# Outputs in two places beside the ring, stored four images at a time, in a group-norm and masked batch-norm kernel on one core

## The chip, the cores and the metric

The kernel runs on one core of a Trainium2 chip. A core has TensorE (PE), VectorE (DVE), ScalarE (ACT), GpSimd (POOL) and SyncE (SP), each with an instruction queue of its own, and 16 DMA engines that all queues share. Here SyncE issues the loads and ScalarE the stores. The metric is the device time of one execution in microseconds (us); lower is better.

## What is computed

The input x is 16 images x 64 channels x 256 x 256, float32, 268 MB. The reference, cut to what matters:

```
def _gn(v, G=32, eps=1e-5):            # mean and variance over each image's group of two channels
    ...
    return ((g - m) / jnp.sqrt(s + eps)).reshape(v.shape)

def _L0_conv_ref(x):                   # masked batch norm, the mean is not subtracted
    x1 = x.sum(axis=1)                 # sum over the 64 channels
    m = x1 != 0
    mean = (sum over images and places where m) / total
    var = (sum of (x - mean)^2 where m) / total
    inv = 1.0 / jnp.sqrt(var + 1e-3)
    out = jnp.where(m[:, None, :, :], x * inv, x)
    ...

x = x + _L0_conv_ref(_gn(x))
```

So each element becomes x plus its group-normed value times a number of its channel, if the sum over all 64 normed channels at its pixel isn't zero. The kernel writes outputs as if no sum were zero, counts the zeros beside it, and has a general path behind a branch (`general`, and its parts on the other engines) for the case that there are any. With these inputs the branch isn't taken.

## The kernel before

**Units and tiles.** The work is cut into 32 units, one for each group of two channels, over all 16 images. In SBUF a unit stands as 128 partitions (2 channels x 64 pieces of the picture) x 16 images x 1024 elements. A tile is four images of a unit, 2 MB. A unit has four tiles (`UNIT_TILES`), loaded in four DMAs and stored in four. There are 128 tiles.

**The ring.** `slots` has ten places of a tile. The first eight (`RING`) hold the tiles in turn, so two units at a time; tile j is in place j % 8. An output is written over its input (`out_in_ring`), except for the first four images of the last unit, which go to place 8 (`APART_PLACE`). Place 9 holds the map of zeros of the last unit. Otherwise the two places are not used in the main path.

**The engines' work on a unit u:**
- SyncE (`load`, L249) loads tile after tile. From the ninth on it waits until the store of the tile eight before it, which stood in the same place, has landed (`stored`). At the end it stores the last unit, image by image (L265 to 267).
- VectorE takes the statistics of every block of 512 elements (`block_stats`, L511), then makes means, scales and biases (`statistics`). Between the steps of that chain it does the first six blocks of the next unit (`meanwhile`), so the chain waits also for the next unit's first tile. The chain passes through small matmuls on PE (L420, L430, L431) and two square roots on ScalarE (L388, L390), and ends with `out_scale` and `out_bias`.
- TensorE (`channel_sums`) adds up the normed channels at each pixel. For 12 of the 16 images the sum goes to one of three banks of PSUM (`flush`), for 4 it stays in PSUM over all units (`stay`).
- ScalarE (`unit` at L386) goes image by image: `take` (L373) copies a flush bank to SBUF, `put_out` (L376) makes the output of an image, and after the first image of the next tile `store` (L382) issues the DMA of the tile before. It waits for an image's sum before it makes the output in place, since TensorE reads the input.
- GpSimd makes the weights and adds up what `take` copied (L349).

All loops are written out by hand, two units a turn, and each engine's order is that of its own code; semaphores hold them together. `out_ready` counts outputs, `image_summed` counts TensorE's sums, `taken` the takes.

Of the kernel before, what the change touches and what calls it, by code (L numbers as in the profile page):

```python
# [16 lines left out]
BLK = 512  # L17
HALVES = 2
TILE_IMAGES = 4
RING = 8  # L20
PLACES = 10
# [4 lines left out]
LAP = 2  # L26


def norm_conv_kernel(nc: bass.Bass, x: bass.AP, out: bass.AP):
# [52 lines left out]
    with ctx:  # L82
# [6 lines left out]
        def sem(name):  # L89
# [46 lines left out]

        APART_PLACE, NOT_ZERO = RING, RING + 1
        not_zero = slots[:, NOT_ZERO * TILE_N:NOT_ZERO * TILE_N + B * BLK // 4].bitcast(U8).rearrange(
            "p (k n) -> p k n", k=B)
# [18 lines left out]
        stored = [sem(f"stored{i}") for i in range(RING)]  # L158
# [13 lines left out]
        out_ready = sem("out_ready")  # L172
        counted = sem("counted")
# [36 lines left out]
        def out_in_ring(u, i):  # L210
            return in_place(APART_PLACE)[:, i, :] if u == LAST and i < APART else image_in_ring(u, i)
# [7 lines left out]
        def wait_for_sum(engine, u, i, it=None):  # L219


            engine.wait_ge(image_summed, in_turn((u * B + sum_order(u).index(i) + 1) * BLOCKS, it, B * BLOCKS))

        def bank_of(u, i):
            return flush[(u * ADDS + flush_order(u).index(i)) % FLUSH_BANKS][:, :]
# [4 lines left out]
        def wait_for_bank(engine, u, i, it=None):  # L230


            if u < LAST:
                engine.wait_ge(taken, in_turn(taken_with(u, i), it, ADDS))
            else:
                engine.wait_ge(compared, flush_order(u).index(i) + 1)

        def wait_for_all_stores(engine):
            for j in range(TILES - RING, TILES - UNIT_TILES):
                engine.wait_ge(stored[j % RING], 16 * (j // RING + 1))  # L240
# [5 lines left out]
        def _(sp):  # L246

            def load(j, it=None):
                if j >= RING:  # L249
                    sp.wait_ge(stored[j % RING], 16 * (j // RING) if it is None else it * 16 + 16 * (j // RING))  # L250
# [9 lines left out]
            sp.wait_ge(stored[(TILES - 1) % RING], 16 * ((TILES - 1) // RING))  # L260
# [4 lines left out]
            for i in range(B):  # L265
                sp.wait_ge(out_ready, LAST * B + i + 1)
                sp.dma_start(out_rows[LAST, :, i, :], out_in_ring(LAST, i)).then_inc(last_stored, 16)
# [34 lines left out]
        def _(pool):  # L302
# [23 lines left out]
            def unit(u, it=None):  # L326
# [9 lines left out]
                for part in sorted(parts, key=lambda part: sum_order(u).index(part[0])):  # L336
# [410 lines left out]
```

## Time and profile before

| | before |
|---|---|
| median of 3 runs | 1353.27 us |
| lowest and highest | 1345.78 and 1357.33 us |
| the profiled execution, its time | 1357.61 us |
| its span, first to last instruction | 1355.9 us |
| busy: DVE, ACT, PE, POOL | 58%, 60%, 54%, 40% of the span |
| loads | 127 DMAs of 2048 KB, median 14.2 us from issue to landing |
| stores from ScalarE | 124 DMAs of 2048 KB, median 14.7 us |
| stores of the last unit, from SyncE | 16 DMAs of 512 KB, median 5.0 us |

The busy share of an engine is the time in which it worked on something. For the DMA engines, "9" in a slice means that they were busy for 90% of it or more; that says nothing of how fast they moved, which the row of GB/s tells. "From issue to landing" includes the time in which a DMA stands in the queue behind others.

### The profile page before, as it was taken

Reading aid. Unit: us, or ns where it says so; the run is one execution under the profiler, and the core shown is the slowest. Engines: PE = TensorE matmul, PEld = TensorE weight load, DVE = VectorE, ACT = ScalarE, POOL = GpSimd, SP = SyncE. Lnnn points to the kernel's source line nnn. Section 1 sums busy time; section 2 is a strip of 40 time slices with the busy share of each in tenths; the row PEclk is TensorE's granted clock in tenths of the full one; section 3 lists DMA queues with packets and bytes.
Section 4 is the critical chain, followed back from the end, with each engine's and each line's share of the span. In section 5 each row is a group of like instructions: output and inputs, shape, how many; then the busy total and the mean of one; then the engine's idle time right before and its main releaser. Section 6 shows DMA issues by size and latency. Waiting matters only on the chain.

```text
span 1355.9 us, 13270 instructions
## 1 busy us (share of the span) xinstructions
PE 736.0 (54%) x2882; PEld 295.1 (22%) x2882; DVE 780.4 (58%) x1892; ACT 816.5 (60%) x950; POOL 547.1 (40%) x568
## 2 busy tenths in 40 slices
PE   0666345654556545466454664446645366535566
PEld 0222111221212222122111222112222122212222
DVE  7566554655546555466654665545765357555474
ACT  0775457654577545675456764567645576546766
POOL 0053344443444434454343543435434354334441
PEclk9987678876787767887667886778767787667888
DMA  9899999999999999999999999999999999999998
GB/s 378 344 404 398 421 392 394 391 394 419 390 396 388 393 420 403 397 389 396 420 392 398 399 403 413 393 396 389 397 420 388 392 384 398 389 421 389 401 416 338
DMA packets 135418, 536.99 MB, mean 396 GB/s; under 512 B 4336, under 2 KB 4336, under 8 KB 135408
## 3 DMA queue, kind: packets, MB, share of 16 engines
q1 hardware_dynamic: 69936, 276.83, 52.8%
q10 hardware_dynamic: 65472, 260.05, 47.4%
q8 instruction: 3, 0.05, 0.0%
q14 instruction: 7, 0.06, 0.0%
HBM read 268.44 MB, written 268.44 MB: 396 GB/s over the span
## 4 chain that ended last, share of the span: by engine, by line
DMA 58%; PE 17%; issue 9%; DVE 7%; ACT 6%; SPq 1%; DVEq 0%; ACTq 0%
DMA slots<-in_x_dram 33%; DMA out_dram<-slots 25%; PE flush L456 9%; ACT slots L376 5%; PE small_ps L420 3%; ACT fresh L373 1%; PE stay L452 1%; PE small_ps L430 1%; PE stay L453 1%; PE small_ps L431 1%; DVE stats L511 1%; DVE dev L556 1%; DVE by_image L541 1%; DVE spread L530 1%; DVE dev L528 1%
## 5 line engine op out<-in xcount | busy, mean ns | idle before, releaser
L511 DVE BATCH_NORM_STATS2 stats<-slots 128x6 f32<-128x512 f32 x1024 | 630.7, 679 | 522.4 <-DMA slots<-in_x_dram 519.4
L376 ACT ACTIVATE slots<-slots,out_bias,out_scale 128x1024 f32<-128x1024 f32 x512 | 622.4, 1246 | 1.6 <-DVE out_bias L567 1.3
L349 POOL TENSOR_TENSOR sums<-fresh,sums 128x512 f32<-128x512 f32 x360 | 459.5, 1276 | 333.5 <-ACT fresh L373 333.5
L456 PE MATMUL flush<-slots,weights 128*64 128x512 f32 x1536 | 441.8, 696 | 40.2 <-ACT fresh L373 39.0
L373 ACT ACTIVATE fresh<-flush,group_bias 128x512 f32<-128x512 f32 x360 | 247.6, 688 | 52.7 <-PE flush L456 52.7
L420 PE MATMUL small_ps<-spread,group_avg 128*128 128x64 f32 x64 | 21.8, 443 | 380.4 <-DVE spread L530 380.4
L388 ACT ACTIVATE by_image<-by_image,eps 128x16 f32<-128x16 f32 x32 | 9.8, 307 | 325.3 <-DVE by_image L534 324.5
L456 PEld LDWEIGHTS flush<-slots,weights 128*64 128x64 f32 x1536 | 128.6, 156 | 296.9 <-issue 149.9
L329 POOL COPY group_mean<-mean_now 128x16 f32 (+1 forms) x32 | 7.0, 220 | 448.4 <-DVE group_bias L547 448.4
L452 PE MATMUL stay<-slots,weights 128*64 128x512 f32 x512 | 139.1, 605 | 0.0
L453 PE MATMUL stay<-minus_mean,weights 128*64 128x512 f32 x512 | 138.1, 593 | 0.0
L420 PEld LDWEIGHTS small_ps<-spread,group_avg 128*128 128x128 f32 x64 | 15.8, 307 | 385.7 <-DVE spread L530 385.7
L390 ACT ACTIVATE col<-small_ps,eps 128x1 f32<-128x1 f32 x32 | 8.4, 261 | 149.8 <-PE small_ps L431 149.8
L323 POOL TENSOR_TENSOR weights<-pair_sum,rstd_now 128x256 f32<-128x256 f32 (+1 forms) x128 | 74.4, 608 | 0.0
L453 PEld LDWEIGHTS stay<-minus_mean,weights 128*64 128x64 f32 x512 | 49.4, 137 | 61.1 <-issue 61.1
L452 PEld LDWEIGHTS stay<-slots,weights 128*64 128x64 f32 x512 | 44.5, 141 | 82.0 <-issue 82.0
L420 PE MATMUL small_ps<-col,chan_avg 128*128 128x1 f32 x64 | 18.8, 362 | 74.2 <-DVE dev L494 74.2
L420 PE MATMUL small_ps<-stats,group_avg 128*128 128x64 f32 x64 | 16.0, 338 | 72.5 <-DVEq L523 72.5
L430 PE MATMUL small_ps<-col,chan_avg 128*128 128x1 f32 x64 | 18.7, 362 | 45.0 <-DVE spread L494 45.0
L420 PEld LDWEIGHTS small_ps<-col,chan_avg 128*128 128x128 f32 x64 | 16.0, 311 | 80.2 <-DVE dev L494 80.2
L420 PEld LDWEIGHTS small_ps<-stats,group_avg 128*128 128x128 f32 x64 | 10.8, 212 | 98.7 <-DVEq L523 56.5
L430 PEld LDWEIGHTS small_ps<-col,chan_avg 128*128 128x128 f32 x64 | 16.0, 310 | 47.8 <-DVE spread L494 47.8
(54 smaller groups left out, 244.6 us busy)
## 6 DMA issues: line engine op xcount, KB each, us to landing
slots<-in_x_dram SPq DMA_DIRECT2D x127, 2048.0 KB, 14.2
out_dram<-slots ACTq DMA_DIRECT2D x124, 2048.0 KB, 14.7
out_dram<-slots SPq DMA_DIRECT2D x16, 512.0 KB, 5.0
slots<-in_x_dram SPq DMA_DIRECT2D x4, 512.0 KB, 6.9
```

What stands on the lines that cost most here:

```text
L323: return pool.tensor_tensor(weights[:, u % 2, first:first + n, :], matrix.unsqueeze(1).to_broadcast([P, n, ROWS]), rstd_now[:, u % 2, firs ...
L349: pool.tensor_tensor(into, fresh[:, k % FRESH_BUFS, :], into, ALU.add).then_inc(added, 1)
L373: nc.scalar.activation(into, bank_of(u, i), ACT.Identity, bias=group_bias[:, u % 2, i:i + 1]).then_inc(taken, 1)
L376: nc.scalar.activation(out_in_ring(u, i), image_in_ring(u, i), ACT.Identity, bias=out_bias[:, u % 2, i:i + 1], scale=out_scale[:, u % 2, i ...
L420: nc.tensor.matmul(out_, lhsT, rhs, start=True, stop=True).then_inc(small_out, 1)
L430: nc.tensor.matmul(bn_var_ps, chan_avg[:, :], var_sum, start=True, stop=False)
L431: nc.tensor.matmul(bn_var_ps, chan_avg[:, :], shifted_sum, start=False, stop=True).then_inc(small_out, 1)
L452: nc.tensor.matmul(into, weight, source, start=u == 0, stop=False)
L453: nc.tensor.matmul(into, weight, minus_mean[:, u % 2, i:i + 1].to_broadcast([P, BLK]), start=False, stop=u == LAST).then_inc(image_summed, 1)
L456: nc.tensor.matmul(into, weight, source, start=True, stop=True).then_inc(image_summed, 1)
L511: last = V.bn_stats(stats[:, u % 2, k * BLOCK_STATS:(k + 1) * BLOCK_STATS], source)
L528: link(V.tensor_tensor(dev[:, :, :], means, over_folds(mean), ALU.subtract))
```

## The change

The ring of eight places stays for inputs alone. Places 8 and 9 become two output places of four images each (`out_places`). `put_out` of units 0 to 30 writes there: images 0 to 3 and 8 to 11 of each unit to the one, 4 to 7 and 12 to 15 to the other. Before the first image of four, ScalarE waits until the store that was issued last from that place has landed (`wait_for_out_places`). `store` sends one output place to HBM, again four images, 2 MB. A new semaphore `tile_free` counts the tiles whose outputs are made and whose sums are done; ScalarE raises it in `free`, right behind the store, and the load waits for it and no longer for a store. `put_out` comes ahead of `take`, as it need not wait for the sum any more.

In the last unit, outputs of images 0 to 13 go to the ring places of the unit before, and 14 and 15 to the first output place. The map of zeros moves to ring space of the unit before, and VectorE begins to count once all outputs of the units before are made. The last unit's order of images, which was 4 to 15 and then 0 to 3, becomes 0 to 15.

The core of the diff:

```diff
+STORE_IMAGES = 4
...
-    APART = TILE_IMAGES
-
-    def sum_order(u):
-        return list(range(B)) if u < LAST else list(range(APART, B)) + list(range(APART))
-
-    def flush_order(u):
-        return [i for i in sum_order(u) if i in flushed]
+    OUT_PLACES = (PLACES - RING) * TILE_IMAGES // STORE_IMAGES
+    UNIT_STORES = B // STORE_IMAGES
+    USES = UNIT_STORES // OUT_PLACES
+    ASIDE = B - 2
...
-        def out_in_ring(u, i):
-            return in_place(APART_PLACE)[:, i, :] if u == LAST and i < APART else image_in_ring(u, i)
+        def out_places(k):
+            at = RING * TILE_N + k * STORE_IMAGES * N
+            return slots[:, at:at + STORE_IMAGES * N].rearrange("p (i n) -> p i n", i=STORE_IMAGES)
+
+        def out_place(u, i):
+            if u < LAST:
+                return out_places(i // STORE_IMAGES % OUT_PLACES)[:, i % STORE_IMAGES, :]
+            return out_places(0)[:, i - ASIDE, :] if i >= ASIDE else image_in_ring(LAST - 1, i)
...
+            def wait_for_place(j, it=None):
+                sp.wait_ge(tile_free, in_turn(j - RING + 1, it, UNIT_TILES))
+
             def load(j, it=None):
                 if j >= RING:
-                    sp.wait_ge(stored[j % RING], 16 * (j // RING) if it is None else it * 16 + 16 * (j // RING))
+                    wait_for_place(j, it)
                 sp.dma_start(in_ring(j), in_dram(x_rows, j, it)).then_inc(loaded[j % RING], 16)
...
-            def store(u, t, it):
-                j = u * UNIT_TILES + t
-                act.wait_ge(out_ready, in_turn((j + 1) * TILE_IMAGES, it, B))
-                act.dma_start(in_dram(out_rows, j, it), in_ring(j)).then_inc(stored[j % RING], 16)
+            def wait_for_out_places(u, k, it):
+                n = u * UNIT_STORES + k
+                if n >= OUT_PLACES:
+                    act.wait_ge(stored[k % OUT_PLACES], in_turn(16 * (n // OUT_PLACES), it, 16 * USES))
+
+            def store(u, k, it):
+                act.wait_ge(out_ready, in_turn(u * B + (k + 1) * STORE_IMAGES, it, B))
+                at = slice(k * STORE_IMAGES, (k + 1) * STORE_IMAGES)
+                if it is None:
+                    into = out_rows[u, :, at, :]
+                else:
+                    into = out_rows[bass.ds(it * LAP + u, 1), :, at, :].rearrange("o p i n -> (o p) i n")
+                act.dma_start(into, out_places(k % OUT_PLACES)).then_inc(stored[k % OUT_PLACES], 16)
+
+            def free(u, t, it):
+                wait_for_sum(act, u, (t + 1) * TILE_IMAGES - 1, it)
+                act.sem_inc(tile_free, 1)
...
                 act.wait_ge(scale_ready, in_turn((u + 1) * 2, it, 2))
+                if u == LAST:
+                    wait_for_sum(act, LAST - 1, B - 1)
                 for i in range(B):
-                    if u < LAST or i >= APART:
+                    if u < LAST and i % STORE_IMAGES == 0:
+                        wait_for_out_places(u, i // STORE_IMAGES, it)
+                    if u == LAST and i == ASIDE:
+                        act.wait_ge(stored[0], 16 * LAST * USES)
+                    put_out(u, i)
+                    if u < LAST and i in flushed:
                         wait_for_sum(act, u, i, it)
-                    if u < LAST and i in flushed:
                         take(u, i, it)
-                    put_out(u, i)
+                    if u < LAST and i and i % STORE_IMAGES == 0:
+                        store(u, i // STORE_IMAGES - 1, it)
                     if u < LAST and i and i % TILE_IMAGES == 0:
-                        store(u, i // TILE_IMAGES - 1, it)
+                        free(u, i // TILE_IMAGES - 1, it)
                 if u < LAST:
-                    store(u, UNIT_TILES - 1, it)
+                    store(u, UNIT_STORES - 1, it)
+                    free(u, UNIT_TILES - 1, it)
...
+            dve.wait_ge(out_ready, LAST * B)
+            for i in range(B):
                 count(i)
```

How the instructions stand on ScalarE, inside the loop over units, from the fourth image of a unit to the first image's neighbour after the store. `slots<-slots` is `put_out`, `fresh<-flush` is `take`; rows without an operation on data (ISA, REGISTER_ALU) compute or hold a wait. Before:

```order
L376 ACTIVATE slots<-slots,out_bias,out_scale 128x1024 [waits image_summed]
L222 REGISTER_ALU
L372 REGISTER_ALU [waits image_summed]
L373 ACTIVATE fresh<-flush,group_bias 128x512 [waits added]
L376 ACTIVATE slots<-slots,out_bias,out_scale 128x1024
L381 ISA
L382 ISA [waits out_ready]
L382 DMA out_dram<-slots 128x4x1024
```

And in the changed kernel, at the same place:

```order
L389 ACTIVATE slots<-slots,out_bias,out_scale 128x1024
L389 ACTIVATE slots<-slots,out_bias,out_scale 128x1024 [waits stored1]
L230 REGISTER_ALU
L385 REGISTER_ALU [waits image_summed]
L386 ACTIVATE fresh<-flush,group_bias 128x512 [waits added]
L400 ISA
L406 ISA [waits out_ready]
L406 DMA out_dram<-slots 128x4x1024
L230 REGISTER_ALU
L389 ACTIVATE slots<-slots,out_bias,out_scale 128x1024 [waits image_summed]
```

The output of the fifth image has moved ahead of its take and has a wait for `stored1` on it; the DMA of the first four images stands behind both. The same rows come again with `stored0` after the eighth image and with `stored1` after the twelfth.

On SyncE, the first two loads of a turn of the loop before:

```order
L251 ISA [waits stored0]
L251 DMA slots<-in_x_dram 128x4x1024
L251 ISA [waits stored1]
L251 DMA slots<-in_x_dram 128x4x1024
```

And in the changed kernel:

```order
L264 ISA [waits tile_free]
L264 DMA slots<-in_x_dram 128x4x1024
L259 REGISTER_ALU
L264 ISA [waits tile_free]
L264 DMA slots<-in_x_dram 128x4x1024
```

The loads stand in the same order, each behind a wait for ScalarE's `tile_free` where a wait for the store of its place was.

## Rows read from the trace of the kernel before

**Rows 1.** The page, busy time by engine and the slices of the span.

```profile
span 1355.9 us, 13270 instructions
PE 736.0 (54%) x2882; PEld 295.1 (22%) x2882; DVE 780.4 (58%) x1892; ACT 816.5 (60%) x950; POOL 547.1 (40%) x568
...
DMA  9899999999999999999999999999999999999998
...
DMA packets 135418, 536.99 MB, mean 396 GB/s; under 512 B 4336, under 2 KB 4336, under 8 KB 135408
```

**Rows 2.** Waits, who for whom: total us, times, longest; SyncE's queue last.

```profile
DVE stats L511 <- DMA slots<-in_x_dram: 519.4, 80, 14.9
...
SPq L251 <- DMA out_dram<-slots: 1199.2, 119, 26.8
```

**Rows 3.** The chain that ended last: start us, us, what; ten of its pieces.

```profile
45.61 6.64 DMA out_dram<-slots
52.44 14.85 DMA slots<-in_x_dram
...
83.53 10.28 DMA out_dram<-slots
93.99 14.94 DMA slots<-in_x_dram
...
125.13 13.72 DMA out_dram<-slots
...
506.99 9.29 DMA out_dram<-slots
516.45 13.78 DMA slots<-in_x_dram
...
546.76 13.49 DMA out_dram<-slots
560.43 14.44 DMA slots<-in_x_dram
...
591.29 9.53 DMA out_dram<-slots
```

**Rows 4.** Busy time in seven stretches; last columns: PE clock, DMA share, GB/s.

```profile
45.60:1305.70 1260.10, 690.98 (x2704) 276.08 (x2702) 717.42 (x1741) 770.72 (x901) 528.43 (x531) 0.75 1.01 398
46.50:51.90 5.40, 5.40 (x28) 2.39 (x27) 5.40 (x10) 5.40 (x7) 0.00 (x0) 1.00 0.97 388
52.80:57.30 4.50, 3.34 (x16) 0.82 (x14) 1.32 (x3) 4.50 (x6) 0.00 (x0) 1.00 1.01 338
86.00:88.40 2.40, 2.40 (x13) 0.89 (x10) 2.10 (x4) 2.40 (x4) 1.97 (x2) 1.00 1.02 331
511.00:519.00 8.00, 6.75 (x32) 2.07 (x31) 4.99 (x9) 8.00 (x9) 5.10 (x4) 1.00 1.03 419
524.00:544.00 20.00, 8.43 (x24) 3.85 (x26) 12.71 (x40) 6.22 (x10) 5.97 (x9) 0.50 1.02 417
546.90:551.00 4.10, 4.10 (x22) 1.77 (x20) 3.62 (x7) 4.10 (x6) 2.88 (x3) 1.00 0.99 281
```

**Rows 5.** Timeline, DMA issues and activations: start us, us, engine line.

```profile
51.86 0.38 ACTq L382 DMA_DIRECT2D out_dram<-slots  x1
...
58.11 0.38 ACTq L382 DMA_DIRECT2D out_dram<-slots  x1
...
83.53 0.40 ACTq L382 DMA_DIRECT2D out_dram<-slots  x1
...
84.10 0.37 SPq L251 DMA_DIRECT2D slots<-in_x_dram  x1
...
89.75 0.39 ACTq L382 DMA_DIRECT2D out_dram<-slots  x1
...
1305.66 0.38 ACTq L382 DMA_DIRECT2D out_dram<-slots  x1
...
1324.40 0.38 ACTq L382 DMA_DIRECT2D out_dram<-slots  x1
...
1330.38 4.64 ACT L376 ACTIVATE slots<-slots,out_bias,out_scale 128x1024 f32<-128x1024 f32 x4 [1.25 <-DVE out_bias L567]
```

**Rows 6.** DMA issues at 51.86, 58.11, 84.10 and 89.75: last column, us to landing.

```profile
out_dram<-slots ACTq DMA_DIRECT2D x1, 2048.0 KB, 9.1
...
out_dram<-slots ACTq DMA_DIRECT2D x1, 2048.0 KB, 15.0
...
slots<-in_x_dram SPq DMA_DIRECT2D x1, 2048.0 KB, 14.4
...
out_dram<-slots ACTq DMA_DIRECT2D x1, 2048.0 KB, 15.1
```

More of the change, by code:

```diff
@@ L157, in norm_conv_kernel @@
         loaded = [sem(f"loaded{i}") for i in range(RING)]
-        stored = [sem(f"stored{i}") for i in range(RING)]
+        stored = [sem(f"stored{i}") for i in range(OUT_PLACES)]
         summed = sem("summed")
@@ L172, in norm_conv_kernel @@
         out_ready = sem("out_ready")
+        tile_free = sem("tile_free")
         counted = sem("counted")
@@ L219, in wait_for_sum @@
         def wait_for_sum(engine, u, i, it=None):
[L222 removed]
+            engine.wait_ge(image_summed, in_turn((u * B + i + 1) * BLOCKS, it, B * BLOCKS))
         def bank_of(u, i):
[L225 removed]
+            return flush[(u * ADDS + flushed.index(i)) % FLUSH_BANKS][:, :]
         def taken_with(u, i):
@@ L235, in wait_for_bank @@
             else:
-                engine.wait_ge(compared, flush_order(u).index(i) + 1)
+                engine.wait_ge(compared, flushed.index(i) + 1)
         def wait_for_all_stores(engine):
-            for j in range(TILES - RING, TILES - UNIT_TILES):
-                engine.wait_ge(stored[j % RING], 16 * (j // RING + 1))
+            for k in range(OUT_PLACES):
+                engine.wait_ge(stored[k], 16 * LAST * USES)
             engine.wait_ge(last_stored, 16 * B)
@@ L259, in _ @@
                 load(j)
-            sp.wait_ge(stored[(TILES - 1) % RING], 16 * ((TILES - 1) // RING))
+            wait_for_place(TILES - 1)
             for i in range(TILE_IMAGES):
@@ L335, in unit @@
                 parts = [list(range(w * EVERY, (w + 1) * EVERY)) for w in range(WEIGHT_PARTS)]
-                for part in sorted(parts, key=lambda part: sum_order(u).index(part[0])):
+                for part in sorted(parts, key=lambda part: part[0]):
                     if u < LAST:
@@ L433, in channel_sums @@
             def channel_sums(u, it=None):
-                for at, i in enumerate(sum_order(u)):
+                for at, i in enumerate(range(B)):
                     if u < LAST:
@@ L446, in channel_sums @@
                             before = (m - FLUSH_BANKS) // ADDS
-                            wait_for_bank(pe, before, flush_order(before)[(m - FLUSH_BANKS) % ADDS], it)
+                            wait_for_bank(pe, before, flushed[(m - FLUSH_BANKS) % ADDS], it)
                     for k in range(BLOCKS):
@@ L605, in count @@
                                            accum_out=n_part[:, i:i + 1]).then_inc(compared, 1)
-            for i in sum_order(LAST):
+            dve.wait_ge(out_ready, LAST * B)
+            for i in range(B):
                 count(i)
```

12 lines of the change are left out of this document (6 added, 6 removed).

## The prediction

> **What bounds the kernel now.** I read the page's busy rows first [rows 1]: no compute engine is busy for more than 60% of the span, while the 16 DMA engines show 9 tenths in nearly every slice. They move 536.99 MB in 1355.9 us, 396 GB/s. The windows say what they can do [rows 4]: 417 GB/s in 524 to 544 us, with loads and stores in flight together, 419 in 511 to 519 with stores alone, but 398 over the 1260.1 us from the first store of unit 0 to the first store of unit 30. So the DMA engines are always busy and run 4 to 5% below what they reach at best. Those 1260.1 us are 30 units, **42.00 us a unit**. A unit loads 8.39 MB and stores 8.39 MB; at 417 GB/s that is 40.2 us.
>
> The waits and the chain show what paces it [rows 2, 3]. VectorE waits 519.4 us for loads. SyncE's queue waits 1199.2 us for stores: a load may only go when the store of the same place, two units older, has landed. The chain is the same ring each time: store out (9.29 us from issue to landing), load in (13.78), about 16.5 us of statistics and first outputs, the next store at 546.76. That is 39.8 us; the next turn has 13.49 and 14.44 us and takes 44.5. Their mean is the 42 us.
>
> **What the change takes away.** The store leaves this ring. A load now waits for `tile_free`, which ScalarE raises when a tile's outputs are made. The old ring would then be 14 + 16.5, some 31 us a unit, and bounds nothing. The bytes, the number of DMAs and the activations stay as they are, so below 40.2 us a unit there is nothing to win: a bound of 30 x 1.8 = 54 us.
>
> **What it adds.** Outputs go to two places, and `put_out` of a tile's first image waits until the store before last has landed. The order listing of ScalarE shows more: the row that waits for `stored1` (or `stored0`) stands ahead of the previous tile's DMA. Call a unit's stores A, B, C, D. B isn't issued until A has landed, C not until B has landed, and the next unit's A not until D has landed. Only D can be queued behind C, since no first image lies between them. Queued behind each waiting activation are the takes (so the PSUM banks), the store and the `tile_free` of the tile before; PE and GpSimd wait with it, but both are ahead by then, and the load is let go only some 0.6 us after the store. So each store starts on an empty queue with a load issued right behind it.
>
> The trace of before has two such pairs. At 83.53 a store goes out, at 84.10 a load [rows 5]: the store lands 10.28 us after its issue, the load 14.4 [rows 3, 6]. At 51.86 a store, at 52.44 a load: 9.1 and 14.85 us [rows 3, 5, 6]. A store alone takes 6.64 (at 45.61) [rows 3]. The reason isn't only the sharing. While the store is alone and the load behind it hasn't begun, the rate is 338 and 331 GB/s (52.8 to 57.3, 86.0 to 88.4), against 388 for the lone store with nothing behind it; 281 is seen for a load with a store issued behind it [rows 4]. So a start of one queue close behind that of the other slows the first, and this happened here in a few places and will now happen three times a unit.
>
> **The sum for a unit.**
> - A to B: 10.28 to land, and 0.35 (my choice) until the store is issued. The old release of SyncE took 93.99 - 93.81 = 0.18 us [rows 3]; ScalarE has the activation, a take and register work to dispatch first, all from its queue. Together 10.6. ScalarE's own work for a tile, 6.25 us (83.53 to 89.75, [rows 5]), lies beside it.
> - B to C: the same, 10.6. In both the last load's tail is still in flight, as a tail was at 83.53, so I take 10.28 rather than 9.1.
> - C to the next A: D is issued some 6.2 us after C and follows it. The pair of before, 83.53 and 89.75: the second lands 15.1 us after its issue, 21.3 after the first's [rows 5, 6]; the other, 51.86 and 58.11, gives 6.25 + 15.0 = 21.3. With 0.35: 21.7.
> Sum **42.9 us**. Beside it ScalarE's way: D's issue, 6.0 us from there to the first activation of the next unit (1324.40 to 1330.38, [rows 5]) and four outputs with their takes, 6.2: from C to A at least 18.5, so 3 us of slack. DVE and PE need only the first load of the next unit but one, which lands 15 us after A, and have 12 us to spare.
>
> Bytes as a cross-check: 16.78 MB in 42.9 us is 391 GB/s, so the DMA engines would not be full, as three stretches of some 3 to 4 us at 331 instead of 417 GB/s cost 2 to 3 us.
>
> **Ends.** The first store is 0.3 us earlier at most (`put_out` no longer waits for the sum). The last unit but one has no loads: A to B about 8, B to C 7.0 (6.64 + 0.35), C to D 6.25; then as before 31.5 us from D's issue (1324.40) to the end. That is 52.75 against 1355.9 - 1305.66 = 50.2 [rows 5]: +2.5. The last unit's outputs go into ring places whose old contents have been stored from elsewhere, so they wait for nothing new except two images for a store long landed: 0.
>
> Whole: 30 x (42.9 - 42.0) + 2.5 = **+29.5 us**. The profiled execution had a span of 1355.9 and a time of 1357.61; the median of the three runs is 1353.27, and the difference carries over: 1353.3 + 29.5 = **1383 us**.
>
> A weighing by the notes, apart from the sum. The Trainium skill, "DMA: Bandwidth & Descriptors", section "Anatomy of one DMA", gives a fixed cost of some 2.0 us for each DMA, mostly completion, and its "Rules for kernel authors" say to issue early and wait late so that the fixed cost overlaps; the change does the opposite for three stores in four. An estimate by that page, with each store sharing the rate half and half from its first byte: 2.0 + 9.6 for A and for B, 2.0 + 19.2 for C and D, which gives 45.5 us a unit and some 1460 us for the whole. The rows give less, 10.28 instead of 11.6, because the load behind starts only some 5 us after the store. The lone store, 6.64 us, does agree with the page (6.8), a page's figure for the other issue path.
>
> **Bounds.** A and B at the friendlier pair: 9.1 + 0.35 each makes the unit 40.55, and the whole 1353.3 - 43.5 + 2.5 = 1312. Above: stores whose start falls just behind a load's, like the one at 125.13, land after 13.72 us [rows 3]; if A and B were all like that, the unit is 49.8 and the whole 1353.3 + 234 + 2.5 = 1590.
>
> **Rivals.**
> 1. The DMA engines stay full (faster). If a store and the load behind it share at the full rate from the start, or the load's tails fill what the store leaves, the unit goes to 40.2: 1353.3 - 54 + 2.5 = 1302; with the friendlier pair 1312. It decides below 41.5 us a unit. For it: 417 and 419 GB/s in long stretches, and the old ring's cost is really gone. Against: the 331, 338 and 281 at each close start. Chance 0.22. The Trainium skill, same page, section "Issuing engines are not separate DMA queues", is on this side: DMAs of the two queues interleave on the same engines, and the issuing engine makes little difference; it has no slow start in it. By that the time is this rival's.
> 2. A standstill: between 41.5 and 42.35 us a unit, the gain of the freed ring and the cost of unqueued stores cancel, 1340 to 1367. Two near-equal figures (9.1 and 10.28) are all that separates it from the others. Chance 0.20.
> 3. The forecast: 42.4 to 45 us a unit, 1367 to 1446, likeliest 1383. Chance 0.51.
> 4. Stores that start behind a load (the 13.72 case) for A and B, up to 1590. It needs the load's issue ahead of the store's, and the program has it behind. Chance 0.07.
>
> A difference of 1% is about what a measurement of this kernel can tell from none. From these: faster 0.22, same 0.20, slower 0.58. The range reaches from above the friendlier pair's 1312 to 1420 (44.1 us a unit): below and above it I leave about a tenth each. The likeliest case's own is 1367 to 1420.
>
> **What would show it.** A store is issued some 0.3 us after the landing of the one before, three times in a unit; ScalarE waits at `put_out` for stores, 3 to 5 us at each tile; DVE's wait for loads all but goes; SyncE's queue waits for ScalarE, not for stores. Stores A and B land in 10 to 10.6 us, D 21.3 after C's issue. Rates of 330 before a load's start and 417 after it. Wrong would be: landings of 9 us or less for A and B (rival 1), more than 12 (rival 4), or the load in front of its store.

## The result and the profile after

The changed kernel is slower: 1395.8 us median (1393.0 to 1397.5, 4 runs) against 1353.7 (1345.8 to 1357.3, 4 runs), a ratio of 1.032 with a 95% interval of 1.027 to 1.037. The profiled execution has a span of 1395.8 us, 39.9 more than before. The forecast was 1383, +29.5. Times below are medians of 4 runs if nothing else is said.

The page of the kernel after, the rows that answer to [rows 1], and the DMA issues with their medians from issue to landing:

```profile
span 1395.8 us, 13521 instructions
PE 783.2 (56%) x2882; PEld 280.5 (20%) x2882; DVE 788.8 (57%) x1892; ACT 826.1 (59%) x950; POOL 545.3 (39%) x568
...
DMA packets 135419, 537.00 MB, mean 385 GB/s; under 512 B 4336, under 2 KB 4336, under 8 KB 135408
...
DMA 76%; ACT 11%; PE 5%; issue 4%; ACTq 2%; DVE 1%; SPq 0%; DVEq 0%
...
slots<-in_x_dram SPq DMA_DIRECT2D x127, 2048.0 KB, 14.5
out_dram<-slots ACTq DMA_DIRECT2D x124, 2048.0 KB, 9.5
```

The same bytes go at 385 GB/s instead of 396. A store now lands in 9.5 us (median) where it took 14.7: there is seldom one queued ahead of it. That is not a gain, it is the queue standing empty.

The waits of the kernel after (who for whom: total us, times, longest), with SyncE's queue last, to set against [rows 2]:

```profile
ACT slots L389 <- DMA out_dram<-slots: 312.0, 92, 7.0
...
DVE stats L548 <- DMA slots<-in_x_dram: 167.1, 35, 6.7
...
SPq L264 <- ACTq L412: 1223.7, 119, 20.2
```

VectorE's wait for loads has fallen from 519.4 to 167.1 us, and SyncE waits for ScalarE, no more for stores: the old ring is gone. In its place ScalarE waits 312 us for stores at `put_out`, which it did not do at all before.

The chain of the kernel after over one unit (start us, us, what), to set against [rows 3]:

```profile
523.10 8.68 DMA out_dram<-slots
...
532.18 12.46 DMA out_dram<-slots
...
545.03 0.38 ACTq L406
...
551.17 15.01 DMA out_dram<-slots
...
566.58 8.83 DMA out_dram<-slots
```

These are the stores A, B, (C at 545.03, then ScalarE's outputs), D, and the next A. Of the 43.5 us of this unit, 36.2 are the landing of A, B and D (8.68, 12.46 and 15.01). There is no load in it any more.

ScalarE's timeline in the same unit (start us, us, engine line, and in brackets the idle time before it and who ended it):

```profile
522.71 1.24 ACT L389 ACTIVATE slots<-slots,out_bias,out_scale 128x1024 f32<-128x1024 f32 x1 [0.86 <-DMA out_dram<-slots]
523.10 0.38 ACTq L406 DMA_DIRECT2D out_dram<-slots  x1
...
531.81 1.24 ACT L389 ACTIVATE slots<-slots,out_bias,out_scale 128x1024 f32<-128x1024 f32 x1 [2.73 <-DMA out_dram<-slots]
532.18 0.38 ACTq L406 DMA_DIRECT2D out_dram<-slots  x1
...
544.66 1.24 ACT L389 ACTIVATE slots<-slots,out_bias,out_scale 128x1024 f32<-128x1024 f32 x1 [6.50 <-DMA out_dram<-slots]
545.03 0.38 ACTq L406 DMA_DIRECT2D out_dram<-slots  x1
...
551.17 0.38 ACTq L406 DMA_DIRECT2D out_dram<-slots  x1
...
558.43 1.24 ACT L389 ACTIVATE slots<-slots,out_bias,out_scale 128x1024 f32<-128x1024 f32 x1 [1.25 <-DVE out_bias L604]
...
566.21 1.24 ACT L389 ACTIVATE slots<-slots,out_bias,out_scale 128x1024 f32<-128x1024 f32 x1 [1.42 <-DMA out_dram<-slots]
```

A, B and C are each issued 0.37 to 0.39 us after the first output of the next tile has begun, and that output was let go by the landing of the store before. D (551.17) waits for no landing.

Windows of the kernel after (last columns: PE clock, DMA share, GB/s): the unit, a stretch in which B and its load are both in flight, and one in which C is alone and its load has been issued but hasn't begun:

```profile
523.10:566.60 43.50, 25.24 (x92) 8.67 (x90) 24.64 (x59) 26.00 (x31) 17.93 (x18) 0.76 0.99 386
535.60:544.00 8.40, 6.01 (x20) 1.68 (x18) 3.21 (x10) 2.56 (x3) 2.42 (x2) 0.80 1.02 422
545.90:550.60 4.70, 0.00 (x0) 0.00 (x0) 0.00 (x0) 4.70 (x7) 3.08 (x3) 0.50 1.01 343
```

All three show the DMA engines as busy throughout. 422 and 343 GB/s are the same "busy".

### The profile page after: what moved, and what is told of

Its sections match the earlier page's. It is cut to its first block, busy times and chain, and to the rows that moved or that the text cites. A ratio compares the mean times of both kernels' runs of the same rounds, so it can differ in the third digit from the quotient of the medians.

```text
span 1395.8 us, 13521 instructions
## 1 busy us (share of the span) xinstructions
PE 783.2 (56%) x2882; PEld 280.5 (20%) x2882; DVE 788.8 (57%) x1892; ACT 826.1 (59%) x950; POOL 545.3 (39%) x568
## 4 chain that ended last, share of the span: by engine, by line
DMA 76%; ACT 11%; PE 5%; issue 4%; ACTq 2%; DVE 1%; SPq 0%; DVEq 0%
DMA out_dram<-slots 74%; ACT slots L389 8%; PE flush L493 3%; ACT fresh L386 3%; DMA slots<-in_x_dram 2%; ACTq L406 2%; PE stay L489 1%; PE stay L490 0%; ACTq L385 0%; SPq L264 0%; ACTq L400 0%; PE small_ps L457 0%; ACT sums L386 0%; PE small_ps L467 0%; DVE dev L593 0%
## 5 line engine op out<-in xcount | busy, mean ns | idle before, releaser
L389 ACT ACTIVATE slots<-slots,out_bias,out_scale 128x1024 f32<-128x1024 f32 x512 | 630.3, 1234 | 353.3 <-DMA out_dram<-slots 312.0
L548 DVE BATCH_NORM_STATS2 stats<-slots 128x6 f32<-128x512 f32 x1024 | 625.7, 679 | 169.6 <-DMA slots<-in_x_dram 167.1
L493 PE MATMUL flush<-slots,weights 128*64 128x512 f32 x1536 | 489.6, 762 | 149.7 <-ACT fresh L386 145.2
L386 ACT ACTIVATE fresh<-flush,group_bias 128x512 f32<-128x512 f32 x360 | 241.4, 671 | 0.0
L493 PEld LDWEIGHTS flush<-slots,weights 128*64 128x64 f32 x1536 | 120.0, 165 | 460.2 <-ACT fresh L386 327.9
L578 DVE RECIPROCAL by_image<-by_image 128x16 f32<-128x16 f32 x32 | 8.1, 252 | 256.4 <-ACT by_image L417 256.4
L563 DVE TENSOR_REDUCE mean_now<-small_ps 128x16 f32<-128x64 f32 x32 | 7.2, 224 | 140.1 <-PE small_ps L457 140.1
L457 PE MATMUL small_ps<-spread,group_avg 128*128 128x64 f32 x64 | 14.2, 304 | 39.7 <-DVE spread L567 39.7
L457 PE MATMUL small_ps<-stats,group_avg 128*128 128x64 f32 x64 | 14.7, 316 | 29.2 <-DVEq L560 29.2
```

What stands on the lines that cost most here:

```text
L386: nc.scalar.activation(into, bank_of(u, i), ACT.Identity, bias=group_bias[:, u % 2, i:i + 1]).then_inc(taken, 1)
L389: nc.scalar.activation(out_place(u, i), image_in_ring(u, i), ACT.Identity, bias=out_bias[:, u % 2, i:i + 1], scale=out_scale[:, u % 2, i:i ...
L457: nc.tensor.matmul(out_, lhsT, rhs, start=True, stop=True).then_inc(small_out, 1)
L493: nc.tensor.matmul(into, weight, source, start=True, stop=True).then_inc(image_summed, 1)
L548: last = V.bn_stats(stats[:, u % 2, k * BLOCK_STATS:(k + 1) * BLOCK_STATS], source)
```

## The experiments

All lengths of a unit below are the mean over the 30 units from the first store of unit 0 to the first store of unit 30 in the profiled execution. Before it is 42.00 us, after 43.29. In both kernels four images are one tile, 2 MB.

**1. The store ahead of the wait.** If the harm is that a store stands behind the wait for the next place, moving it ahead should take the harm away.

```diff
                 for i in range(B):
+                    if u < LAST and i and i % STORE_IMAGES == 0:
+                        store(u, i // STORE_IMAGES - 1, it)
                     if u < LAST and i % STORE_IMAGES == 0:
                         wait_for_out_places(u, i // STORE_IMAGES, it)
                     ...
-                    if u < LAST and i and i % STORE_IMAGES == 0:
-                        store(u, i // STORE_IMAGES - 1, it)
```

> The changed kernel with one thing moved: ScalarE issues the store of a full place before it waits for the next place, instead of behind that wait and the first output and take of the next tile. Theory 1 (stores go out unqueued because each waits for the landing of the one before; every start on an empty queue, with a load close behind, runs slow): two stores stand in the queue, one follows the other without a gap, a unit takes 40.2 to 41 us instead of 43.3, about 1310 to 1330 us in all, faster than the kernel before (1354). Theory 2 (the two places are too few whatever the order: ScalarE is stopped by the landing of the store before last): B can be made only 10 us after A's issue in either order, the unit stays at 43 us, about 1390. Theory 3 (loads let go by tile_free crowd the stores, and in the old kernel the wait for stores kept them apart): no change from 1396.

Measured: 1377.2 us, ratio to before 1.015 (1.012 to 1.019), 42.57 us a unit. It gains 0.7 us a unit, not 2 to 3, and stays 1.5% above the kernel before. The number lies between the theories, nearer to the second and third, and the trace shows why. ScalarE's timeline of this version:

```profile
507.94 1.24 ACT L389 ACTIVATE slots<-slots,out_bias,out_scale 128x1024 f32<-128x1024 f32 x1 [1.33 <-DVE out_bias L604]
...
514.47 0.38 ACTq L406 DMA_DIRECT2D out_dram<-slots  x1
...
521.42 0.38 ACTq L406 DMA_DIRECT2D out_dram<-slots  x1
...
529.70 0.38 ACTq L406 DMA_DIRECT2D out_dram<-slots  x1
536.30 1.24 ACT L389 ACTIVATE slots<-slots,out_bias,out_scale 128x1024 f32<-128x1024 f32 x1 [6.76 <-DMA out_dram<-slots]
...
542.81 0.38 ACTq L406 DMA_DIRECT2D out_dram<-slots  x1
```

A and B are now queued together, and C behind them. But D's outputs (at 536.30) need B's place, and B lands 21.8 us after A's issue. Then come D's outputs (6.5), the statistics of the next unit (D's issue to the first output, 7.65 at 500.29 to 507.94) and A's outputs (6.5). In the mean of 30 units it is 22.2 us to the landing of B, 6.5 from there to D's issue and 13.9 from D's issue to the next A's, which is the 42.57: a new ring, and at its end the store queue moves nothing for a moment (here A's first packet comes 1.7 us after D's last).

**2. Store and `tile_free` ahead.** The same, with the load let go as well.

```diff
+                    if u < LAST and i and i % STORE_IMAGES == 0:
+                        store(u, i // STORE_IMAGES - 1, it)
+                    if u < LAST and i and i % TILE_IMAGES == 0:
+                        free(u, i // TILE_IMAGES - 1, it)
                     if u < LAST and i % STORE_IMAGES == 0:
                         wait_for_out_places(u, i // STORE_IMAGES, it)
                     ...
-                    if u < LAST and i and i % STORE_IMAGES == 0:
-                        store(u, i // STORE_IMAGES - 1, it)
-                    if u < LAST and i and i % TILE_IMAGES == 0:
-                        free(u, i // TILE_IMAGES - 1, it)
```

> As the one before, and tile_free too is raised ahead of the wait for the next place, so that the load is let go as soon as the outputs of its tile are made. Theory 1: the load isn't late in either, since a unit's loads have 12 us to spare; 40.2 to 41 us a unit, 1305 to 1330 us, within 0.5% of the one before. Theory 2: about 1390. Theory 3 (loads crowd the stores): slower than the one before by 1% or more, since loads come earlier.

Measured: 1378.5 us, 42.53 us a unit, the same as the one before. C's load now goes 0.7 us behind its store instead of 7.6, and the time stays: loads that come earlier do not crowd the stores here, and theory 3 falls.

**3. Idle time in the ring.** To show that the ring of experiment 1 is what bounds it, eight idle activations of 128x16, 1.85 us together (528.44 to 530.29 in the trace), were put ahead of the first output of each unit.

```diff
                 act.wait_ge(scale_ready, in_turn((u + 1) * 2, it, 2))
+                for k in range(8):
+                    if u * 8 + k:
+                        act.wait_ge(idled, in_turn(u * 8 + k, it, 8))
+                    nc.scalar.activation(idle[:, :], group_avg[:, 0:16], ACT.Identity).then_inc(idled, 1)
```

> The version with the store ahead of the wait (1377 us, 42.55 us a unit) and eight small idle activations, together some 2.5 to 3 us, ahead of the first output of each unit. It tests the ring that I now see there: store A issued, B behind it lands some 21.5 us later, then D's outputs (6.6), the statistics' way through ScalarE (7.5), A's outputs (6.1), next A. If that ring bounds it, all of the idle time comes on top: 45 to 45.6 us a unit, 1450 to 1470 us. If the DMA engines' rate or the landing of D bounds it, the idle time is hidden: under 1400.

Measured (2 runs): 1435.1 us, 44.42 us a unit. The idle time was shorter than the 2.5 to 3 us that I had said, so the time missed my range, and all of it came on top: 44.42 - 42.57 = 1.85. The ring bounds that version.

The same edit to the changed kernel:

> The changed kernel with the same 1.85 us of idle activations ahead of each unit's first output as in the version with the store ahead, where all of it came on top (42.57 to 44.42 us a unit). Here ScalarE waits 1.4 us at the fifth output for the landing of D, so the landing of D, not ScalarE's way, should end last: only 0.4 to 0.6 us a unit on top, 1405 to 1415 us. If ScalarE's way bounds this kernel too: 1.85 us a unit, about 1451 us.

Measured (2 runs): 1415.8 us, 43.85 us a unit, 0.56 more. There the landing of D ends last and hides 1.3 of the 1.85 us, as the 1.42 us of idle at 566.21 say. So the changed kernel is bound by the landings of its stores, with ScalarE's way close behind. That also explains experiment 1: once B is queued behind A, the ring that goes through ScalarE's outputs of D and A and the statistics is the next bound, only 0.7 us further on.

**4. Four places of two images.** The output places keep their 4 MB but are cut finer.

```diff
-STORE_IMAGES = 4
+STORE_IMAGES = 2
```

> The changed kernel with STORE_IMAGES = 2: four output places of two images each, 1 MB a store, order as it is. The store of a place still stands behind the wait for the next place, but that wait is for the store three before, so up to three stores are in the queue. Theory 1: queue never empty while ScalarE has outputs, 40.5 to 41.5 us a unit, 1310 to 1340 us, although the stores are twice as many. Theory 2 (too little room for outputs): the room is the same 4 MB, so no better than 1380. Theory 3: 1396, or more with smaller DMAs.

Measured: 1303.5 us, ratio to before 0.961 (0.957 to 0.964), **40.18 us a unit**, better than the range that I gave. Slices of the page of this kernel, GB/s:

```profile
GB/s 376 389 421 420 421 421 421 421 421 421 421 421 417 421 421 406 421 419 416 420 411 421 408 421 420 413 421 399 421 420 421 421 403 421 408 419 421 420 395 307
```

And its waits for stores and for loads, and the issues with the median us to landing:

```profile
ACT slots L389 <- DMA out_dram<-slots: 213.2, 133, 2.1
DVE stats L548 <- DMA slots<-in_x_dram: 192.3, 52, 6.8
...
out_dram<-slots ACTq DMA_DIRECT2D x248, 1024.0 KB, 14.8
```

ScalarE still waits 133 times, but at most 2.1 us at a time, and half as large a store takes longer to land (14.8 against 9.5) because there is always another ahead of it. From the first and last packet of each DMA in the traces, between 200 and 1100 us, one can work out how long both queues had data in flight: 98% of the time here, 67% in experiment 1, 56% in the changed kernel, 61% before. (The share alone doesn't rank kernels: experiment 2 has 78% and is no faster than experiment 1, and experiment 7 will have 68% and be nearly as fast as this one.) The room was never too small; it was cut too coarsely. Of two places of 2 MB one is being emptied for 9 to 15 us, during which ScalarE can fill only the other.

**5. Finer still.** `STORE_IMAGES = 1`, eight places of one image; the last two outputs go to the first two places.

```diff
-STORE_IMAGES = 4
+STORE_IMAGES = 1
...
-            return out_places(0)[:, i - ASIDE, :] if i >= ASIDE else image_in_ring(LAST - 1, i)
+            return out_places(i - ASIDE)[:, 0, :] if i >= ASIDE else image_in_ring(LAST - 1, i)
```

> The changed kernel with STORE_IMAGES = 1: eight output places of one image, 512 KB a store, 496 stores instead of 124, the order otherwise as it is. Theory 1a (what matters is that the store queue is never empty; with two images it wasn't for 98% of the time and the rate was 418 GB/s): no more to win, 40.2 us a unit, 1295 to 1310 us, the same as with two images (1303.5). Theory 1b (finer is better without end): under 1290. Rival (the many small DMAs cost rate): 1320 or more.

Measured: 1305.1 us, 40.22 us a unit. No more to win, and nothing lost to 496 stores of 512 KB.

**6. Two images and both ahead.** Experiments 2 and 4 together.

> Two images a store, and store and tile_free ahead of the wait for the next place (the two earlier edits together). With the DMA engines full already, the order has nothing left to give: 1298 to 1308 us, within 0.5% of 1303.5. If the order still cost something there, 1290 or less.

Measured: 1307.5 us, 40.23 us a unit. The order has nothing to give once the places are fine enough.

**7. In place, but stored by halves.** This parts the size of the stores from the separate places. It is the kernel before, with two stores a tile (`PARTS` is 2; the counts of `stored` that others wait for are doubled with it).

```diff
+PARTS = 2
...
-            def store(u, t, it):
-                j = u * UNIT_TILES + t
-                act.wait_ge(out_ready, in_turn((j + 1) * TILE_IMAGES, it, B))
-                act.dma_start(in_dram(out_rows, j, it), in_ring(j)).then_inc(stored[j % RING], 16)
+            HALF_TILE = TILE_IMAGES // PARTS
+
+            def store(u, n, it):
+                j = u * UNIT_TILES + n // PARTS
+                first = n % PARTS * HALF_TILE
+                act.wait_ge(out_ready, in_turn(u * B + (n + 1) * HALF_TILE, it, B))
+                into = in_dram(out_rows, j, it)[:, first:first + HALF_TILE, :]
+                act.dma_start(into, in_ring(j)[:, first:first + HALF_TILE, :]).then_inc(stored[j % RING], 16)
...
-                    if u < LAST and i and i % TILE_IMAGES == 0:
-                        store(u, i // TILE_IMAGES - 1, it)
+                    if u < LAST and i and i % HALF_TILE == 0:
+                        store(u, i // HALF_TILE - 1, it)
```

> The kernel before (outputs in place, loads wait for stores) with one thing changed: each tile is stored in two DMAs of two images, the first issued some 3.4 us before the second. It parts smaller stores from separate places. If the smaller stores alone were the gain of the version with two images, this gives about 1303 as well. If the loads' wait for stores still bounds it: the ring of 42 us loses at most the 3.4 us by which half the tile goes earlier, 40.2 to 41.5 us a unit, 1310 to 1345 us. If the ring is bound by the landing of the last image whatever its size: no change, 1354.

Measured: 1310.7 us, ratio 0.966 (0.961 to 0.972), 40.48 us a unit. Its chain (start us, us, what), three turns, and a window (last columns: PE clock, DMA share, GB/s):

```profile
488.00 10.29 DMA out_dram<-slots
498.45 14.54 DMA slots<-in_x_dram
...
529.20 9.91 DMA out_dram<-slots
539.29 14.06 DMA slots<-in_x_dram
...
570.08 9.69 DMA out_dram<-slots
...
610.72 9.41 DMA out_dram<-slots
```

```profile
200.00:1100.00 900.00, 513.44 (x2020) 205.15 (x2018) 540.42 (x1291) 573.65 (x671) 400.49 (x401) 0.76 1.02 414
```

It is the ring of [rows 3], but the store in it takes 9.4 to 10.3 us in each turn, where before it was 9.3 in one and 13.5 in the next. The half that goes 3 us earlier has opened the queue, and the last half follows it: in the packets, the half issued at 488.00 begins as the one issued at 485.24 ends, at 494 us. So smaller stores give nearly the whole gain with no separate places at all. With two images a store, the separate places give 0.961 against 0.966, and the intervals overlap: what they add cannot be told from nothing here.

This also shows where the rate is lost. The store queue of this version moves nothing for 16% of the time, and both queues have data in flight for only 68%, yet it moves 414 GB/s against 417 in experiment 4 (200 to 1100 us). By the packets, a DMA that is alone with nothing issued behind it runs at 421 GB/s here and at 401 in the kernel before. What costs is the stretch in which one queue moves and the DMA issued on the other hasn't begun: it makes up 37% of the changed kernel's time, at 365 GB/s, and 18% of the kernel before, at 350, but here 18% at 395. Why a start costs less beside stores of 1 MB, no run shows.

**8. When the load goes.** Three attempts at the pair itself. First, `tile_free` raised three images later:

```diff
-                    if u < LAST and i and i % TILE_IMAGES == 0:
+                    if u < LAST and i > TILE_IMAGES and i % TILE_IMAGES == 3:
                         free(u, i // TILE_IMAGES - 1, it)
```

> The changed kernel with tile_free raised three images later (for the last tile of a unit at the same place as before), so that a load is issued some 5 us behind the store and not 0.7. Loads have slack, so this shows what the close start costs the store. Theory 1: store A alone lands in about 7 us instead of 8.9; the load is then 1 to 2 us ahead of B, whose start falls behind it (first byte some 4 us after issue, landing 12 to 13): the unit stays within 43 to 45 us, 1390 to 1450 us, and the low rate of 330 GB/s moves from the stores' starts to the loads' starts. If only the closeness of the two mattered and not the empty queue, the unit would fall to 41 to 42 us, 1330 to 1355.

Measured: 1433.7 us, 44.54 us a unit. But the edit did not do what it should: the load went 1.1 us behind the store, not 5, as ScalarE's queue runs ahead of its engine and reached `tile_free` early. Even these 0.4 us cost 1.25 us a unit: A lands 0.4 us sooner (8.4 us after its issue in the mean of 30 units), so that B is issued closer behind the start of A's load; in the packets B begins 3.6 us after its issue instead of 2.6, and it lands after 13.5 us instead of 12.1. So I had it wait for the fourth output as well:

```diff
-                    if u < LAST and i and i % TILE_IMAGES == 0:
+                    if u < LAST and i > TILE_IMAGES and i % TILE_IMAGES == 3:
+                        act.wait_ge(out_ready, in_turn(u * B + i + 1, it, B))
                         free(u, i // TILE_IMAGES - 1, it)
```

> The changed kernel with tile_free of the first three tiles of a unit held back until the fourth output of the next tile is made, so that the load is issued some 5.5 us behind the store (in the earlier try it came only 0.4 us later, since ScalarE's queue runs ahead of its engine). If the close start of the load is what slows the stores A, B, C: each lands after about 7 to 8.5 us instead of 8.9 and 12.5, the unit takes 40 to 42 us, 1310 to 1350 us. If only the total of the traffic counts, or if the late load then catches the next store's start: 43 to 45 us, 1390 to 1450 us.

Measured: 1440.4 us, 44.74 us a unit. Its chain (start us, us, what) and a window while its load is alone, with store B issued behind it at 544.19:

```profile
534.37 9.48 DMA out_dram<-slots
...
544.19 12.07 DMA out_dram<-slots
...
562.95 15.01 DMA out_dram<-slots
```

```profile
542.90:548.40 5.50, 2.52 (x8) 0.49 (x8) 0.19 (x1) 4.52 (x5) 2.12 (x2) 0.80 0.94 296
```

The later load does not spare the stores; it only moves the slow start: now the load runs at 296 GB/s while B waits to begin. In the mean of 30 units A lands after 9.0 us (8.8 in the changed kernel) and B after 13.5 (12.1). The hope of 40 to 42 us fell, the other reading held.

Then the pair turned round: `tile_free` first, and the store only when SyncE has issued the load (a semaphore `let_go`).

```diff
+            def free_first(u, t, it):
+                act.wait_ge(out_ready, in_turn(u * B + (t + 1) * TILE_IMAGES, it, B))
+                free(u, t, it)
+                act.wait_ge(let_go, in_turn(u * UNIT_TILES + t + 1, it, UNIT_TILES))
...
+                    if u < LAST and i and i % TILE_IMAGES == 0:
+                        free_first(u, i // TILE_IMAGES - 1, it)
                     if u < LAST and i and i % STORE_IMAGES == 0:
                         store(u, i // STORE_IMAGES - 1, it)
```

> The changed kernel with the order of the pair turned round: ScalarE raises tile_free first and issues the store only when SyncE has issued the load, some 0.8 us later. If the second of a close pair starts some 4 us late whichever it is (theory 1, the fourth rival of the prediction): stores A and B begin 4.4 us after their issue and land after 12 to 13 us, a unit takes 48 to 52 us, 1530 to 1650 us. If the two only share the rate: the store loses the 0.8 us by which it is issued later, 44 to 46 us a unit, 1420 to 1470 us.

Measured (2 runs): 1678.6 us, 52.6 us a unit. Its chain:

```profile
520.49 12.90 DMA out_dram<-slots
...
534.44 13.38 DMA out_dram<-slots
...
555.06 16.66 DMA out_dram<-slots
```

In both kernels some 0.6 us lie between the two issues, and who is first is worth 9.3 us a unit. About 2 of them are the later issue itself (1.05 us from a landing to the next issue here, 0.4 in the changed kernel, at A, B and D). The rest is in the landings: A, B and C take 13.2, 13.2 and 15.8 us in the mean, where they took 8.8, 12.1 and 9.0, and in this version each begins 4.8 us after its issue. Sharing the rate cannot do that; the fourth rival's mechanism is real, and the changed kernel escapes it, in part, because its load is issued behind its store.

**9. The pair alone.** No computation, only DMAs of 2 MB, each trial from empty queues, in one run with four repetitions. All of the kernel's arithmetic and most of its traffic are left out. The program is a list of such trials on ScalarE and SyncE, for instance:

```
store();  act.sem_inc(go, 1)                            # the load is issued some 0.45 us behind
act.sem_inc(go, 1);  act.wait_ge(let_go, loads);  store()   # the load first
```

> No computation at all: only DMAs of 2 MB between SBUF and HBM, each trial started with both queues empty, four times over: a store alone, a load alone, a store with a load issued right behind it, a load with a store behind it, a store with a load some 4 us behind it, two stores, two loads. All arithmetic of the kernel and most of its traffic are left out. Theory 1 (the close start is a matter of the two queues, not of the engines that work beside it): store alone lands in 6.3 to 6.8 us; with a load behind, the store's data come at 330 GB/s or less until the load begins 4.2 to 4.9 us after the store's issue, and the store lands after 8.5 to 10 us; load first, the same with the roles changed. Rival (the low rate of the start comes from SBUF accesses of the busy engines): the store runs at 385 to 395 GB/s until the load begins and lands after 8 us or less, the load begins within 1 to 1.5 us of its issue.

Its timeline, DMA issues, the first trials of the kinds "store alone", "store, then load" and "load, then store":

```profile
23.91 0.42 ACTq L95 DMA_DIRECT2D out_dram<-slots  x1
...
42.72 0.38 ACTq L95 DMA_DIRECT2D out_dram<-slots  x1
...
57.79 0.38 ACTq L95 DMA_DIRECT2D out_dram<-slots  x1
```

The store at 23.91 is alone, the one at 42.72 has a load 0.45 us behind it, the one at 57.79 a load 0.45 us ahead. How long each takes from issue to landing:

```profile
out_dram<-slots ACTq DMA_DIRECT2D x1, 2048.0 KB, 6.6
...
out_dram<-slots ACTq DMA_DIRECT2D x1, 2048.0 KB, 9.5
...
out_dram<-slots ACTq DMA_DIRECT2D x1, 2048.0 KB, 13.3
```

And the windows (ACT, POOL busy, PE clock, DMA share, GB/s): the lone store; the store before its load begins; both; a load before the store behind it begins:

```profile
24.90:30.10 5.20, 0.81 (x1) 0.00 (x0) 1.00 0.99 398
43.70:47.40 3.70, 0.00 (x0) 0.00 (x0) 1.00 1.02 337
47.60:51.60 4.00, 0.00 (x0) 0.00 (x0) 1.00 1.02 421
58.40:62.70 4.30, 0.00 (x0) 0.00 (x0) 1.00 1.00 260
```

The four repetitions agree within 0.5 us. In the packets, a load behind a store begins 4.3 to 4.4 us after its issue, and a store behind a load 4.7 to 5.0 us after it, where a lone one begins after 0.9 to 1.1. Until then the first runs at 337 (store) or 260 GB/s (load) in the windows shown, 334 to 337 and 250 to 264 in the repetitions. No engine works beside it, so the slow start belongs to the two queues, not to the engines' own accesses. With the load 3.7 us behind, the store lands after 7.4 to 7.7 us, still 0.8 to 1.1 more than alone. Why the second begins so late, and why the first is slow until it does, no run here shows.

## Why the prediction was right, point by point

The time was right, and so was what bounds the changed kernel: stores that go out one at a time and their landings. Two signs that the prediction itself had named as wrong did come, though: A lands after 8.8 us in the mean (9 or less was to speak for rival 1) and B after 12.1 (more than 12, for rival 4), where 10 to 10.6 was forecast for both. Their sum came out near the forecast only because one was too high and the other too low; that part of the hit is luck.

- **What bounds the kernel before**: the ring of store and load, 39.8 and 44.5 us in turn. Right. In its packets, the store of the slower turn (546.76) was issued 1.4 us behind a load and begins 4.2 us after its issue; those of the quicker turns (506.99 and 591.29) were issued 5.2 and 5.3 us behind one and begin after 2.7 and 1.7.
- **Stores one at a time**: right, as the chain shows (B, C and the next A are each issued 0.4 us after the landing before; I had 0.35). D is queued behind C, as I had it. ScalarE's waits for them are 2.7, 6.5 and 1.4 us, not 3 to 5.
- **A to B**, 10.6 us in the sum: measured 9.20 in the mean of 30 units, 8.8 of it to land (8.68 in the unit shown). It is like the friendlier pair (9.1), since at A's issue the last load's tail has only some 1.4 us left.
- **B to C**, 10.6 in the sum: measured 12.56, 12.1 of it to land (12.46 in the unit shown). This term failed. I priced B as a second A. But A's load is in full flight when B is issued: in the unit shown B's first packet comes 2.8 us after its issue instead of 0.9, and its own load begins 1.6 us after that, so B shares the rate over almost its whole length. The errors in A and B (1.4 too much, 2.0 too little) nearly cancel: 21.8 us against 21.2.
- **C to the next A**, 21.7: measured 21.54.
- **The unit**, 42.9: measured 43.29. Thirty units make 11.8 us too little, the ends 1.3 too much; together they are the 10.4 us by which the span was missed (39.9 against 29.5). In the medians it is 12.8 us.
- **Slack of ScalarE's way**, 3 us: measured 1.4. I had taken 6.0 us from D's issue to the next output out of the last unit [rows 5], where VectorE has no blocks of a next unit to do between the steps. In the loop it is 7.3. It hid no error in the time, but it is what stopped experiment 1.
- **Ends**, +2.5: measured 51.8 us from the first store of unit 30 to the end, +1.6, and the first store 0.4 us earlier, so +1.2.
- **Rival 1** (the DMA engines stay full, 1302) is what four places give, 1303.5, and not what two give. Its rate was right and its mechanism was not: a store and a load issued close behind it do not share at the full rate from the start (337 GB/s in experiment 9). Four places reach the rate because almost every DMA is queued behind another, so there are hardly any such starts.
- **Rival 4** needs the load ahead of the store; experiment 8 made it so, with 1678.6, more than the 1590 that I had worked out, because C then starts behind a load too. A milder form of it is in the changed kernel: its B starts while A's load is in flight.
- **The fixed cost by the Trainium skill** ("DMA: Bandwidth & Descriptors", "Anatomy of one DMA"), some 2 us, stands there for DMAs that GpSimd issues. The estimate from it for a lone store, 2.0 + 4.8 = 6.8 us, is near what experiment 9 measures, 6.6. The estimate of 45.5 us a unit by it was too high against the 43.3 measured, and it doesn't tell the pair's two orders apart (9.5 and 13.3 us for the store). The same page of the Trainium skill, section "Issuing engines are not separate DMA queues", has the DMAs of the two queues interleave, whichever engine started them; they do in mid-flight (421 GB/s), but not at a start (337 and 260), where the measurement decides.

What the sign hung on was close: at 42.0 us the unit before was itself 1.8 us above what experiment 4 reaches, and mostly for the same reason, slow starts of one queue beside the other (18% of its time at 350 GB/s). The change took away one cause of such starts and put in another, so that they are 37% of the time.

## What to carry to other kernels

When the DMA engines are shown as busy all the time, read the GB/s beside it, and look for stretches in which one queue moves while a DMA issued on the other hasn't begun. They come where stores or loads start on an empty queue; the share of time in which both move is not enough to tell, as experiment 7 shows. For a store that is issued by the engine that fills the buffers, what counts is less how much room there is than how many pieces it is cut into: with pieces of half the size the kernel keeps one more store queued at every moment, and four pieces of 1 MB gave 7% over two of 2 MB. Before adding a separate output buffer, try smaller stores in place: that is a change of a few lines, and here it gave all but what can't be told from nothing.

## What the runs showed of the hardware

- Two DMAs of 2 MB issued on SyncE's and ScalarE's queues within half a microsecond of each other, both queues empty (experiment 9): the second begins 4.3 to 4.4 us (a load) or 4.7 to 5.0 us (a store) after its issue, where a lone one begins after 0.9 to 1.1, and the first runs until then at 337 GB/s (a store, 398 alone) or 260 GB/s (a load).
- Once both are in flight they reach 421 GB/s together in the window shown, against 398 for the lone store.
- The DMA engines show a busy share of 1.00 to 1.02 at 260, 337, 343 and 422 GB/s alike.
- Stores of 512 KB in a queue that never empties are no slower than stores of 1 MB: 40.22 and 40.18 us a unit.
- ScalarE's queue raises a semaphore well ahead of the activations written before it: in experiment 8 a signal meant to come 5 us later came 0.4 us later, until it waited for their count (then the load went 6.3 us behind the store).
